# A wait of GpSimd in each first norm, one bias loaded as a column, and new orders in a 16 x 256 x 128 attention and FFN kernel

## The reference

```python
def attn(x, ln_g, ln_b, ...):
    n = ln(x, ln_g, ln_b)
    W1 = mlp(n, h1_w1, h1_b1, h1_w2, h1_b2)      # gelu(n @ w1 + b1) @ w2 + b2, 128 -> 512 -> 128
    W2 = mlp(n, h2_w1, h2_b1, h2_w2, h2_b2)
    W3 = tril(einsum('bzn,bsn->bzs', W1, W2))
    t = ln(gelu(einsum('bzs,bsm->bzm', W3, n)), ln_g, ln_b)
    x1 = x + t
    return x + mlp(ln(x1, ln_g, ln_b), fm_w1, fm_b1, fm_w2, fm_b2)

def ffn(x, ...):                                  # w1, w2, h1, h2, w3 hold only -1, 0 and 1
    h = silu(x @ w1.T * s1) * (x @ w2.T * s2)     # 128 -> 512
    h = gelu(h @ h1.T * sh1)                      # 512 -> 512
    h = gelu(h @ h2.T * sh2)                      # 512 -> 512
    return h @ w3.T * s3                          # 512 -> 128

x = x + layernorm(attn(layernorm(x)))
x = x + layernorm(ffn(layernorm(x)))
```

## Time and profile before

| what | value |
|---|---|
| runs | 363.68, 365.59, 365.98 us; median 365.59 |
| span of the profiled execution | 362.6 us |
| PE busy | 350.1 us, 97% |
| PEld busy | 289.2 us, 80% |
| DVE busy | 319.9 us, 88% |
| ACT busy | 305.2 us, 84% |
| POOL busy | 147.2 us, 41% |
| DMA | 9.08 MB moved, mean 25 GB/s |

### The profile page before, as it was taken

One profiled execution on the slowest core, in us unless ns is written; L12 is line 12 of the kernel. 1 busy time (PEld: TensorE's weight loads), 2 busy tenths in 40 slices (PEclk: granted clock), 3 DMA queues, 4 the chain that ended last, 5 costly groups with the idle time before them and its releaser, 6 DMA issues.

```text
span 362.6 us, 6039 instructions
## 1 busy us (share of the span) xinstructions
PE 350.1 (97%) x1788; PEld 289.2 (80%) x1788; DVE 319.9 (88%) x954; ACT 305.2 (84%) x552; POOL 147.2 (41%) x213
## 2 busy tenths in 40 slices
PE   6989999999999999999999999999999999999993
PEld 5867687778888888888888888888888887788992
DVE  5889999999999999889989989998969998886936
ACT  5999999997779979988599888897799569959892
POOL 4168842860546052504750286003920174044411
PEclk9999999999999999999999999999999999999998
DMA  7507020000000000000010001000000001001111
GB/s 233 174 14 245 4 60 1 1 2 1 3 0 0 2 0 2 17 13 2 1 29 3 0 0 33 0 1 2 1 0 2 0 2 31 0 2 29 32 30 33
DMA packets 8804, 9.08 MB, mean 25 GB/s; under 512 B 577, under 2 KB 6722, under 8 KB 8770
## 3 DMA queue, kind: packets, MB, share of 16 engines
q1 hardware_dynamic: 8226, 8.41, 7.7%
...
...
## 4 chain that ended last, share of the span: by engine, by line
PE 67%; ACT 13%; DVE 10%; issue 5%; DMA 2%; POOL 1%; SPq 1%; POOLq 0%; DVEq 0%; ACTq 0%
PE bank L1224 8%; PE bank L1226 8%; PE bank L1240 6%; PE bank L1241 6%; PE bank L1123 4%; PE bank L1104 4%; PE bank L1108 4%; PE bank L1105 4%; PE bank L1120 4%; PE bank L1121 4%; PE bank L1206 4%; PE bank L1209 4%; ACT h_hidden_hi L510 3%; PE bank L1046 2%; ACT bank L515 2%
## 5 line engine op out<-in xcount | busy, mean ns | idle before, releaser
L715 DVE TENSOR_TENSOR ffn_gate_lo<-bank,ffn_gate_hi 128x512 fp32r<-128x512 f32 (+1 forms) x72 | 44.1, 626 | 6.0 <-ACT bank L584 4.9
L510 ACT ACTIVATE h_hidden_hi<-bank,cols 128x512 fp32r<-128x512 f32 x64 | 46.1, 760 | 3.5 <-PE bank L1108 3.2
L515 ACT ACTIVATE bank<-bank,cols 128x512 f32<-128x512 f32 x64 | 45.1, 739 | 0.3
L715 DVE TENSOR_TENSOR h_hidden_lo<-bank,h_hidden_hi 128x512 fp32r<-128x512 f32 x64 | 43.0, 681 | 2.5 <-ACT bank L515 2.5
L584 ACT ACTIVATE bank<-bank,cols 128x512 f32<-128x512 f32 (+1 forms) x72 | 43.7, 620 | 0.7
L1224 PE MATMUL bank<-ffn_gate_hi,ffn_w_hi 128*128 128x512 f32 (+1 forms) x108 | 40.5, 381 | 0.2 <-DVE ffn_gate_lo L715 0.2
L1226 PE MATMUL bank<-ffn_gate_lo,ffn_w_hi 128*128 128x512 f32 (+1 forms) x108 | 39.3, 370 | 0.2 <-DVE ffn_gate_lo L715 0.2
L578 ACT ACTIVATE ffn_h_hi<-bank,cols 128x512 fp32r<-128x512 f32 (+1 forms) x36 | 23.0, 646 | 13.5 <-PE bank L1226 8.3
L578 ACT ACTIVATE ffn_gate_hi<-bank,cols 128x512 fp32r<-128x512 f32 (+1 forms) x36 | 23.2, 647 | 10.6 <-PE bank L1226 8.3
L364 POOL TENSOR_TENSOR XR<-X,ln_x_r 128x512 f32<-128x512 f32 x8 | 8.3, 1042 | 53.6 <-DVE bank L861 53.4
L715 DVE TENSOR_TENSOR ffn_h_lo<-bank,ffn_h_hi 128x512 fp32r<-128x512 f32 (+1 forms) x36 | 22.0, 626 | 8.0 <-ACT bank L584 7.8
...
## 6 DMA issues: line engine op xcount, KB each, us to landing
raw<-ffn_w SPq DMA_DIRECT2D x5, 512.0 KB, 3.9
...
```

The lines of the kernel that those rows point to most:

```text
L510: nc.scalar.activation(dst, bank(f"{L}u{j}", c)[:, :], ACT.Gelu, bias=bias_of(L, j)).then_inc(*hi[L].done(c, j))
L515: nc.scalar.activation(u[:, :], u[:, :], ACT.Gelu, bias=bias_of(L, j)).then_inc(*act2[L].done(c, j))
L715: return nc.vector.tensor_tensor(dst, whole, high.bitcast(f32), ALU.subtract)
```

## The change

Three things change. (1) POOL: after the power in x_s_(c) the engine waits until all four tiles of n_second(c) are done, and then writes one column, `quiet`. DVE's n_first(c) waits for the first instruction of x_s_(c) in place of the statistics. (2) fm_b2 is loaded by a DMA straight into a column, behind the third piece of x and ahead of the FFN pieces; the DMA of the row, the product of one element and the copy go, and fm_evict(0) waits for the load. (3) All eight rows of TURNS and the orders of the four engines are laid anew, with the same calls.

```diff
...
@@ -286,11 +285,11 @@
             attn_piece(0)
             attn_piece(1)
             attn_piece(2)
-            sp.dma_start(b2_row, rows[2:3, :]).then_inc(b2_in, 16)
             x_piece(1, 1, 2)
             for i in (3, 4, 5):
                 attn_piece(i)
             x_piece(2, 2, 3)
+            sp.dma_start(fm_b2[:, :], rows[2:3, :].rearrange("o d -> d o")).then_inc(b2_in, 16)
             for i in (0, 1):
                 sp.wait_ge(*attn_lo.at(0, 2 * i + 1))
                 ffn_piece(i)
@@ -332,6 +331,9 @@
                 pool.wait_ge(*x_scale.at(c, 0))
                 nc.gpsimd.tensor_tensor(x_s[:, :], x_vs[:, :], neg_half[:, :], ALU.pow).then_inc(*x_scale.done(c, 1))
 
+                pool.wait_ge(*n_v_ready.at(c, T - 1))
+                nc.gpsimd.memset(quiet[:, :], 0.0).then_inc(*quiet_over.done(c))
+
             def n_low(c):
                 pool.wait_ge(*n_hi.at(c))
                 nc.gpsimd.tensor_tensor(n_tok[1][:, :, :], NF[:, :, :], n_tok[0][:, :, :].bitcast(f32), ALU.subtract).then_inc(*n_lo.done(c))
...
@@ -542,6 +544,8 @@
             def fm_evict(c):
                 if c:
                     act.wait_ge(*oT.at(c - 1))
+                else:
+                    act.wait_ge(b2_in, 16)
                 act.wait_ge(*down["fm"].at(c, J - 1))
                 nc.scalar.activation(OTA[:, :], bank("fmd", c)[:, :], ACT.Identity, bias=fm_b2[:, :]).then_inc(*fm_out.done(c))
 
...
@@ -725,7 +733,6 @@
 
             def fm_bias_add():
                 dve.wait_ge(*fm_b.at(0))
-                nc.vector.tensor_scalar(fm_b2[:, :], bank("fb", 0)[:, J:J + 1], 1.0, None, ALU.mult)
                 nc.vector.tensor_tensor(fm_bias[:, :], bank("fb", 0)[:, 0:J], cols[:, C_B1["fm"]:C_B1["fm"] + J], ALU.add).then_inc(*fm_b_added.done(0))
 
             def gate_constants():
@@ -764,7 +771,7 @@
                     dve.wait_ge(*n_lo.at(c - 1))
                 else:
                     dve.wait_ge(*rows_ready.at(0))
-                dve.wait_ge(*x_stats.at(c, 1))
+                dve.wait_ge(*x_scale.at(c, 0))
                 for t in range(T):
                     last = nc.vector.scalar_tensor_tensor(NF[:, t, :], X[:, c * T + t, :], mv("x", c)[:, t, 0:1], bc[:, R_G, :], ALU.subtract, ALU.mult)
                 last.then_inc(*n_v.done(c))
...
@@ -1086,9 +1098,7 @@
                 pe.wait_ge(cols_in, 16)
                 for j in range(J):
                     w = ATTN["fmu"] + j * P
-                    nc.tensor.matmul(bank("fb", 0)[:, j:j + 1], raw[:, w:w + P], cols[:, C_B:C_B + 1], start=True, stop=True)
-                pe.wait_ge(b2_in, 16)
-                last = nc.tensor.matmul(bank("fb", 0)[:, J:J + 1], b2_row, ones[0:1, :], start=True, stop=True)
+                    last = nc.tensor.matmul(bank("fb", 0)[:, j:j + 1], raw[:, w:w + P], cols[:, C_B:C_B + 1], start=True, stop=True)
                 last.then_inc(*fm_b.done(0))
 
             def up_mm(L, j, c):
...
```

More of the change, by code:

```diff
@@ L430, in x_end @@
                 nc.gpsimd.tensor_tensor(xc(c), xc(c), FN[:, :, :], ALU.add).then_inc(*x_out.done(c))
-            x_s_(0); n_low(0); x_s_(1); x_s_(2); lo_block(0); lo_block(1); x_r(0); xr_scale(0); lo_block(2); xr_b(0)
-            lo_block(3); n_low(1); t_r(0); x_r(1); lo_block(4); lo_block(5); x1_r(0); lo_block(6); lo_block(7); x_s_(3)
-            lo_block(8); n_low(2); t_r(1); xr_scale(1); xr_b(1); lo_block(9); o_r(0); x_r(2); x1_r(1); lo_block(10); y_r(0)
-            y_centre(0); y_scale(0); o_shift_(0); n_low(3); x_s_(4); xr_scale(2); xr_b(2); o_r(1); t_r(2); x_r(3); x1_r(2)
@@ L441, in _ @@
-            y_scale(5); x1_r(6); xr_scale(7); o_r(6); xr_b(7); t_r(7); y_r(6); y_centre(6); y_scale(6); x1_r(7); f_r(4)
-            x_end(3); o_shift_(6); o_r(7); o_shift_(7); y_r(7); y_centre(7); y_scale(7); f_r(5); x_end(4); x_end(5); x_shift()
-            f_r(6); x_end(6); last_rstd(0); last_rstd(1)
+            x_s_(0); n_low(0); x_s_(1); x_r(0); xr_scale(0); lo_block(0); xr_b(0); lo_block(1); lo_block(2); lo_block(3)
+            n_low(1); x_s_(2); t_r(0); lo_block(4); lo_block(5); x1_r(0); lo_block(6); lo_block(7); lo_block(8); x_r(1)
@@ new lines, in _ @@
+            n_low(2); x_s_(3); t_r(1); xr_scale(1); xr_b(1); o_r(0); lo_block(9); o_shift_(0); lo_block(10); x1_r(1)
+            x_r(2); y_r(0); y_centre(0); y_scale(0); n_low(3); x_s_(4); xr_scale(2); xr_b(2); o_r(1); x_r(3); t_r(2)
+            n_low(4); x1_r(2); y_centre(1); y_r(1); o_shift_(1); y_scale(1); x_s_(5); t_r(3); xr_scale(3); xr_b(3); f_r(0)
+            x1_r(3); o_r(2); x_end(0); x_r(4); y_centre(2); y_r(2); y_scale(2); o_shift_(2); f_r(1); t_r(4); xr_scale(4)
+            xr_b(4); n_low(5); o_r(3); x_end(1); x1_r(4); o_shift_(3); x_s_(6); y_r(3); y_centre(3); y_scale(3); x_r(5)
@@ new lines, in _ @@
+            n_low(6); f_r(2); o_r(4); xr_scale(5); t_r(5); o_shift_(4); xr_b(5); y_centre(4); y_r(4); y_scale(4); x1_r(5)
+            x_r(6); x_s_(7); x_end(2); f_r(3); o_r(5); xr_scale(6); xr_b(6); o_shift_(5); t_r(6); x_end(3); x_r(7); y_r(5)
+            y_centre(5); x1_r(6); n_low(7); y_scale(5); f_r(4); xr_scale(7); o_r(6); xr_b(7); t_r(7); y_r(6); o_shift_(6)
+            y_centre(6); y_scale(6); x1_r(7); x_end(4); o_r(7); y_r(7); y_centre(7); y_scale(7); o_shift_(7); f_r(5)
+            x_end(5); f_r(6); x_shift(); x_end(6); last_rstd(0); last_rstd(1)
@@ new lines, in _ @@
+            up_hi("h1", 2, 1); up_hi("h1", 3, 1); up_act("h1", 2, 1); t_act(0); n_high(1); up_hi("h2", 1, 1)
+            up_act("h1", 3, 1); lo_sum(0); up_act("h2", 1, 1); up_hi("h2", 2, 1); up_hi("h2", 3, 1); up_act("h2", 2, 1)
+            lo_sum(1); nT_high(2); ffn_w_hi(2); up_act("h2", 3, 1); ffn_w_hi(3); down_hi("h1", 1); up_hi("h1", 0, 2)
+            up_hi("h1", 1, 2); up_act("h1", 0, 2); up_act("h1", 1, 2); ffn_w_hi(4); down_hi("h2", 1); up_hi("h1", 2, 2)
+            up_hi("h2", 0, 2); up_act("h1", 2, 2); mT_high(0); up_hi("h1", 3, 2); up_act("h2", 0, 2); score_hi(0, 1)
@@ new lines, in _ @@
+            score_hi(1, 1); up_hi("h2", 1, 2); up_hi("fm", 0, 0); up_act("h2", 1, 2); up_act("h1", 3, 2)
+            up_hi("fm", 1, 0); t_act(1); n_high(2); up_act("fm", 0, 0); lo_sum(2); up_act("fm", 1, 0); up_hi("fm", 2, 0)
+            up_hi("h2", 2, 2); up_hi("fm", 3, 0); up_act("fm", 2, 0); up_act("fm", 3, 0); ffn_w_hi(5); up_act("h2", 2, 2)
+            nT_high(3); fm_evict(0); up_hi("h2", 3, 2); down_hi("h1", 2); up_act("h2", 3, 2); up_hi("h1", 0, 3); lo_sum(3)
+            up_act("h1", 0, 3); up_hi("h1", 1, 3); up_hi("h1", 2, 3); up_act("h1", 1, 3); up_act("h1", 2, 3)
```

552 lines of the change are left out of this document (276 added, 276 removed), and 46 rows, old and new, of the table TURNS.

## The result

The changed kernel takes 368.99 us (median of 4 runs, 368.47 to 369.94) against 364.7 of the kernel before on the same chip. The ratio is 1.0103, with a 95% interval of 1.0071 to 1.0135: slower by about 1%. Its profiled execution has a span of 367.1 us, 4.5 more than before.

What follows compares the result with a forecast made beforehand. It took ACT and DVE to bound 20 to 80 us and TensorE the middle; terms summed to +0.1, rounded to +0.2, giving a 362.8 us span and, 3.0 above it, 365.8 us; range 361.2 to 369.3.

Steps and rivals of the forecast that it cites:

- rival (b): 20 to 80 us: ACT stands 1.8 us for the last FFN piece, passed on to DVE and TensorE; 369.5 us, chance 0.15.
- The middle "has almost nothing to give": 80 to 300 us: PE never stops, so a better order of matmuls can win almost nothing there.
- DVE and ACT order in the head: Up to about 110 us: both engines full and order nearly kept, so no gain; +0.3 us, from −2 to +1.5.
- the instructions stand within a few positions of where they stood: DVE and ACT orders: instructions feeding TensorE up to about 110 us hardly move, and their work is the same.
- The stand-still: POOL waits during the second norm: 0 gain on DVE; first norm of chunk 3 later, +0.1 us, 0 to +0.3.
- Rival (c): The stand-still shields DVE's norms from POOL: at most 1.2 us gained, 364.6 us; chance 0.08.
- The bias: DVE copy of 145 ns leaves the saturated stretch, −0.1 us; the new load lands long before fm_evict near 59 us.
- The last FFN piece: ACT's ffn_w_hi(5) waits 0.4 to 0.5 us for piece 5, loaded after lo_sum(2); +0.5 us, all of it counted.
- The fourth y: y_scale(3) on POOL ends later, so TensorE's transpose of it stalls 0 to 0.7 us; taken as +0.3.
- Late stalls: Chunk 7 transposes of M and OTA, placed behind more matmuls, lose their waits; −1.0 us, from −1.3 to 0.
- if their sources are no later: Condition for the late transposes: added matmuls cover 0.46 and 0.81 us of waiting, together 1.27.
- The other signs: Named: ACT wait 0.3 to 1.8 us, head PEld 44 to 45.5 us, norm steps 348 ns, fm_evict not waiting.

Runs made afterwards that it cites:

- e1_quiet_last: The changed kernel with the one-column tile quiet allocated last, so all later tiles stand at their old addresses; 365.95 us, ratio 1.0025 to the kernel before.
- e2_before_shifted: The kernel before with one unused column allocated behind warm, so all later tiles start 32 bytes higher; 368.87 us, ratio 1.0089.
- e3: e1_quiet_last with gate_constants moved on DVE back behind the statistics of chunk 4, about 50 us; 364.22 us, ratio 0.9971 to the kernel before.

## Why the prediction was right, and where it was wrong

The time, 368.99 us, lies inside the range, at its upper end; the likeliest value of 365.8 was 3.2 us too low. That it is inside is luck. Two of the three largest effects, +3.0 us for the place of the tiles and +1.7 for gate_constants, were in neither the sum nor a rival, and the range reached up to 369.3 for rival (b), a stall on the last FFN piece that did not come up. The sum came near for another kernel, e1_quiet_last (365.95), the same program with its tiles in their old places, and that is chance too: there the loss by gate_constants and the gain of the late stretch, both missing in the sum, cancel in part. The 3.0 us that the sum kept between span and time held two things: in the runs with both on record the time is 1.7 to 1.9 us above the span (368.92 and 367.1), and the rest came from comparing a median with one execution whose landing was short.

- **The middle "has almost nothing to give".** Right for waits, wrong as a bound: it can lose. The sum had no term for the place of tiles, since I read `quiet` in the diff as a column of 4 bytes and not as a shift of all that stands behind it. It measured +3.0 us (368.99 against 365.95; 2.8 by the ratios, and 3.3 by the ratio of e2_before_shifted), and no rival named it.
- **DVE and ACT order in the head, +0.3.** The step "the instructions stand within a few positions of where they stood" failed: gate_constants moved by 22 us. By the rows they are 0.31 us of DVE work, in the new place 2.1. That measured 1.7 us (e3), past the term's own end of +1.5. The rest of the head's order gave back: e3_gate_late has 45.35 us of loads from 20 to 80 us against 44.56 before, 1.0 us won. So the head as a whole lost the 0.7 us of above, inside the term's range, by two errors that cancel in part.
- **The stand-still, 0 to +0.1.** Right in size: 0 to 0.5 us in its favour. The reasoning was only half right. I had read from the norms' spread that DVE is not slowed beside POOL and that POOL alone loses 0.24 us. DVE does lose, by as much as 0.9 us, when its instruction starts while one of POOL's of 128x512 is under way; the one overlap in the earlier trace rows was with a power of 128x4. The earlier trace rows showed none because the old order happened to have no such meeting of a norm. It had one of a weight split, which also reads two inputs in SBUF, and which I had not looked for: 0.94 us beside POOL's block that ended at 24.80, where its kind took 0.69 (median):

```profile
24.41 0.94 DVE L715 TENSOR_TENSOR attn_w_lo<-raw,attn_w_hi 128x512 fp32r<-128x512 f32 x1
```

Rival (c) was the right mechanism, met at gate_constants instead of the norm, where the change has no stand-still.
- **The bias, −0.1.** Right; 0.9992 can't be told from 1.
- **The last FFN piece, +0.5 us.** The mechanism was right and the size too large. The sum began at 53.18 and its read ended at 54.52, SP issued at 54.54, and ACT stood 0.20 us at 58.16:

```profile
53.18 1.25 ACT L478 ACTIVATE raw<-ffn_w_lo 128x1024 f32<-128x1024 f32 x1
54.13 0.39 ACT L478 ACTIVATION_READ_ACCUMULATOR raw<-ffn_w_lo 128x1 f32 x1
58.16 1.06 ACT L472 ACTIVATE ffn_w_hi<-raw 128x1024 fp32r<-128x1024 f32 x1 [0.20 <-DMA raw<-ffn_w]
```

The sum's start to the step took 4.98 us, against 4.9 worked out for the load; but the six instructions between took 0.3 us more than six times 0.57 (54.22 to 57.96). Rival (b) did not come up.
- **The fourth y, +0.3 us.** It cost nothing. POOL ended y_scale(3) at 189.01, the transpose's loads began at 190.83, two microseconds later than the slot that I had counted, and waited for nothing:

```profile
185.13 0.10 POOL L335 MEMSET quiet<- 128x1 f32 x1 [2.71 <-DVE NF L783]
187.97 1.04 POOL L408 TENSOR_TENSOR raw<-raw,ln_y_r 128x512 f32<-128x512 f32 x1
```

```profile
190.83 0.59 PEld L1058 LDWEIGHTS bank<-ident,raw 128*128 128x128 f32 x4
```

- **Late stalls, −1.0 us.** Both waits are gone in the changed kernel, as the sum had it: PEld has no wait over 0.15 us from 300 to 330 us. But the change gained 1.6 us there (2.1 with the tiles in place), and the reason was wrong: the two moves that I had costed make the kernel 0.38% slower when they are made alone. The step that failed is "if their sources are no later": it looked at the two sources and not at what DVE, in order, had queued behind them.

The other signs: ACT stood for the piece, 0.20 us, a little under the 0.3 named; PEld in the head was at 43.96 us, at the edge of the 44 to 45.5 named; the norms took 345 and 346 ns; and the first fm_evict did not wait for the bias.

The steps from before to the change are +3.0 for the place of the tiles, +1.7 for gate_constants, and −1.1 for all the rest (e3_gate_late against before, 364.22 to 365.28). They make the whole of 3.7 us, but for rounding, by construction, each being a difference of neighbours in one chain. The experiments in the kernel before check them from the other side: by the ratios 3.3 us (2.0 to 4.5) for the tiles and 1.3 (0.4 to 2.1) for gate_constants.

The −1.1 is less than what TensorE won. By its loads e3_gate_late is ahead of before by 1.0 us in 20 to 80 us and by 2.1 in 300 to 330, and behind by 0.7 in 80 to 300. At TensorE's last transposes it is ahead by 2.1 us:

```profile
357.16 0.44 PE L1072 MATMUL bank<-ident,raw 128*128 128x128 f32 x2 [0.63 <-ACT raw L590]
```

```profile
355.04 0.44 PE L1085 MATMUL bank<-ident,raw 128*128 128x128 f32 x2 [0.41 <-ACT raw L595]
```

From there on a part is lost again. ACT issues its store 1.7 us sooner (358.58 against 360.27), as DVE's end is 0.4 us longer, and the store lands after 3.9 us instead of 1.9, so that the two spans come out level (362.9 and 362.6). How much of the medians is landing I can't say, since only profiled executions show it.
